# A two-layer graph network on Trainium2: GpSimd asks for free places in the ring of gathered rows by pairs of edge tiles, in place of groups of four

## What is computed

```python
h = X * rsqrt(deg_out)                                  # L0: convolution
agg = segment_sum(h[src], dst, N) * rsqrt(deg_in)
gX = relu(agg @ W) + relu(X @ Wres)
x = layernorm(X + batchnorm(gX))
h = x @ W_enc.T + b_enc                                 # L1: two layers
for l in range(2):
    m = relu(concat([h[src], h[dst]]) @ msg_W1[l].T + msg_b1[l])
    m = m @ msg_W2[l].T + msg_b2[l]
    agg = segment_sum(m, dst, N)
    h = layernorm(h + concat([h, agg]) @ upd_W[l].T + upd_b[l])
out = layernorm(x + h @ W_out.T + b_out)
```

## Time and profile before

| what | value |
| --- | --- |
| median of the three runs | 3993.59 us |
| lowest and highest of them | 3985.41 and 4000.14 us |
| span of the profiled execution (first to last instruction) | 3444.6 us |
| median less the span | 549.0 us |
| PE, PEld, DVE, ACT, POOL busy | 86%, 78%, 78%, 69%, 54% of the span |
| granted TensorE clock, mean | 0.971 |
| first edge stage, from GpSimd's first gather to its last | 544.5 to 1003.4 us |
| second edge stage, likewise | 1577.4 to 2101.3 us |
| third edge stage, likewise | 2532.3 to 3056.9 us |

### The profile page before, as it was taken

One profiled execution on the slowest core, in us unless ns is written; L12 is line 12 of the kernel. 1 busy time (PEld: TensorE's weight loads), 2 busy tenths in 40 slices (PEclk: granted clock), 3 DMA queues, 4 the chain that ended last, 5 costly groups with the idle time before them and its releaser, 6 DMA issues. The chain is left out here.

```text
span 3444.6 us, 92529 instructions
## 1 busy us (share of the span) xinstructions
PE 2975.2 (86%) x25312; PEld 2674.1 (78%) x25312; DVE 2700.0 (78%) x8634; ACT 2379.7 (69%) x5642; POOL 1846.0 (54%) x1782
## 2 busy tenths in 40 slices
PE   4975656777767789997999998999979999989998
PEld 3753334555543378987999998999979999989998
DVE  9999967888856688885777776666657777769998
ACT  3779945777742368886777775666657777759999
POOL 0000036577755533335776776555547767766664
PEclk9999988999979989999999999999989999999999
DMA  0027635777649989997776654999977766548887
GB/s 21 2 69 229 223 103 162 221 219 215 195 139 340 346 280 355 366 356 250 225 221 208 191 158 123 327 327 326 328 239 229 221 210 194 164 129 287 296 295 240
DMA packets 460711, 777.79 MB, mean 226 GB/s; under 512 B 113689, under 2 KB 115865, under 8 KB 460393
## 3 DMA queue, kind: packets, MB, share of 16 engines
q1 hardware_dynamic: 355046, 548.85, 48.2%
q10 hardware_dynamic: 67714, 147.73, 12.5%
q0 software_dynamic: 37632, 77.15, 9.2%
HBM read 451.50 MB, written 321.78 MB: 224 GB/s over the span
## 5 line engine op out<-in xcount | busy, mean ns | idle before, releaser
L883 DVE SCALAR_TENSOR_TENSOR edges_acc<-edges_acc,keep,edges_ps_a 128x128 f32 (+1 forms) x2352 | 820.3, 349 | 272.1 <-issue 145.9
L851 POOL DMA_INDIRECT ring<-table_p,esrc x784 | 787.5, 1004 | 313.3 <-issue 206.0
L1011 PE MATMUL edges_ps_m<-ring,ident 128*128 x3136 | 609.7, 276 | 33.8 <-POOLq L840 33.8
L1012 PE MATMUL edges_ps_m<-edges_q_ring,edges_turned 128*128 x3136 | 608.8, 276 | 0.0
L1011 PEld LDWEIGHTS edges_ps_m<-ring,ident 128*128 128x128 f32 x3136 | 478.6, 193 | 34.7 <-ACT edges_turned L967 17.7
L1012 PEld LDWEIGHTS edges_ps_m<-edges_q_ring,edges_turned 128*128 128x128 f32 x3136 | 478.8, 193 | 0.0
L979 ACT ACTIVATE edges_msg<-edges_ps_m 128x512 f32<-128x512 f32 x392 | 234.2, 597 | 295.5 <-PE edges_ps_m L1012 294.7
L1021 PE MATMUL edges_ps_a<-edges_onehot,edges_msg 128*128 128x128 f32 x3136 | 414.0, 275 | 0.0
L851 POOL DMA_INDIRECT ring<-table_h,esrc x344 | 327.7, 953 | 138.5 <-issue 93.5
L1021 PEld LDWEIGHTS edges_ps_a<-edges_onehot,edges_msg 128*128 128x128 f32 x3136 | 381.7, 192 | 0.0
L868 DVE TENSOR_TENSOR edges_onehot<-iota,drel 128x512 f32<-128x512 f16 x441 | 305.0, 692 | 96.1 <-PE edges_ps_a L1021 94.0
(11 more groups left out here) (315 smaller groups left out, 6776.2 us busy)
## 6 DMA issues: line engine op xcount, KB each, us to landing
table_z<-nodes_z_t SPq DMA_DIRECT2D x196, 256.0 KB, 5.0
table_p<-nodes_p_out SPq DMA_DIRECT2D x196, 256.0 KB
table_q<-nodes_q_out ACTq DMA_DIRECT2D x196, 256.0 KB
edges_q_ring<-table_q SPq DMA_DIRECT2D x196, 256.0 KB, 4.8
edges_d_ring<-table_d ACTq DMA_DIRECT2D x98, 512.0 KB
table_t<-edges_acc SPq DMA_DIRECT2D x196, 256.0 KB
nodes_in_a<-table_t SPq DMA_DIRECT2D x196, 256.0 KB
nodes_in_z<-table_z SPq DMA_DIRECT2D x196, 256.0 KB, 4.3
```

The source lines that it names most:

```text
L851: nc.gpsimd.indirect_dma_start(out=ring[:, e % RE * W:e % RE * W + P], out_offset=None, in_=table[:, :], in_offset=bass.IndirectOffsetOnAx ...
L883: nc.vector.scalar_tensor_tensor(out=to, in0=to, scalar=m.keep[:, s:s + 1], in1=ps_a[:, i % AR, where(j):where(j) + F], op0=ALU.mult, op1= ...
L1011: nc.tensor.matmul(to, m.ident[:], rows[j], start=True, stop=False)
L1012: last = nc.tensor.matmul(to, turned[:, i % QR, j * P:(j + 1) * P], slots[j], start=False, stop=True)
```

## The change

The table holds one number for each pair of edge tiles (`NPAIR` = 196) instead of one for each group of four (98), and is now called `pair_end`. GpSimd waits before each pair, for the pair that holds the same two places, 64 tiles back (`AHEAD`). The words are loaded every 24 pairs. The announcement to TensorE (`landed`) stays as it was, by fours. In `plan_stage` the arrays `bound`, `full`, `tf` and `ends` grow to 196 columns.

```diff
+NPAIR = TP // 2
+PW = -(-NPAIR // 3)
+AHEAD = 64
...
-                nc.gpsimd.iota(bound[:], pattern=[[4 * P, NCHUNK]], base=4 * P, channel_multiplier=0,
+                nc.gpsimd.iota(bound[:], pattern=[[2 * P, NPAIR]], base=2 * P, channel_multiplier=0,
...
-                link(nc.vector.tensor_scalar(tf[:, 0, :], ps_c[0:1, 2, 0:NCHUNK], float(TP - 1), -1.0, ALU.min, ALU.add))
+                link(nc.vector.tensor_scalar(tf[:, 0, :], ps_c[0:1, 2, 0:NPAIR], float(TP - 1), -1.0, ALU.min, ALU.add))
...
-                link(nc.vector.tensor_copy(ends[:, 1, 0:NCHUNK], tf[:, 1, :]))
-                link(nc.vector.tensor_scalar(ends[:, 2, 0:NCHUNK], ends[:, 1, 0:NCHUNK], 2, None, ALU.arith_shift_right))
-                link(nc.vector.tensor_scalar(ends[:, 3, 0:NCHUNK], ends[:, 2, 0:NCHUNK], 1, None, ALU.add))
-                for k, to in ((0, m.chunk_end), (3, m.tile_end)):
-                    pack(to[:, 0:EW], 10, [ends[:, k, :].rearrange("o (w j) -> o w j", j=3)[:, :, j] for j in range(3)], 10)
+                link(nc.vector.tensor_copy(ends[:, 1, 0:NPAIR], tf[:, 1, :]))
+                link(nc.vector.tensor_scalar(ends[:, 2, 0:NPAIR], ends[:, 1, 0:NPAIR], 2, None, ALU.arith_shift_right))
+                link(nc.vector.tensor_scalar(ends[:, 3, 0:NPAIR], ends[:, 2, 0:NPAIR], 1, None, ALU.add))
+                for k, to, w in ((0, m.chunk_end, EW), (3, m.pair_end, PW)):
+                    pack(to[:, 0:w], 10, [ends[:, k, 0:3 * w].rearrange("o (w j) -> o w j", j=3)[:, :, j] for j in range(3)], 10)
...
-                    last = nc.tensor.matmul(ps_c[:, 2, 0:NCHUNK], ones[0:K, :], full[:, k, :], start=k == 0, stop=k == 3)
+                    last = nc.tensor.matmul(ps_c[:, 2, 0:NPAIR], ones[0:K, :], full[:, k, :], start=k == 0, stop=k == 3)
...
                 for g in range(first, NCHUNK):
-                    if g >= RE // 4:
-                        k = g - RE // 4
-                        if k % 24 == 0:
-                            ends = load(mybir.EngineType.Pool, m.tile_end[0:1, k // 3:k // 3 + 8])
-                        pool.wait_ge(s_seg if degrees else s_pq, third(ends, k))
-                        pool.sem_inc(s_go, 1)
-                    for j in range(4):
-                        e = 4 * g + j
+                    for e in range(4 * g, 4 * g + 4):
+                        if e % 2 == 0 and e >= AHEAD:
+                            k = (e - AHEAD) // 2
+                            if k % 24 == 0 or e == 4 * first:
+                                ends = load(mybir.EngineType.Pool, m.pair_end[0:1, k // 24 * 8:k // 24 * 8 + 8])
+                            pool.wait_ge(s_seg if degrees else s_pq, third(ends, k))
+                            pool.sem_inc(s_go, 1)
                         nc.gpsimd.indirect_dma_start(
```

More of the change, by code:

```diff
@@ L529, in plan_stage @@
         cols = sb("cols", [K, 4, 4])
-        bound = sb("bound", [K, NCHUNK])
+        bound = sb("bound", [K, NPAIR])
         cnt_w = sb("cnt_w", [K, 4, P])
         ended, ended1, at_e = sb("ended", [K, 4, S]), sb("ended1", [K, 4, S]), sb("at_e", [K, 4, S], F16)
-        full = sb("full", [K, 4, NCHUNK])
+        full = sb("full", [K, 4, NPAIR])
         local_t = sb("local_t", [K, 4, P], F16)
@@ L537, in plan_stage @@
         ti = sb("ti", [1, 9, S], I32)
-        tf, ends = sb("tf", [1, 3, NCHUNK]), sb("ends", [1, 4, 3 * EW], I32)
+        tf, ends = sb("tf", [1, 2, NPAIR]), sb("ends", [1, 4, 3 * PW], I32)
         ps_c = pb("ps_c", 4)
@@ L621, in _ @@
                 nc.vector.memset(m.chunk_end[:], 0)
-                nc.vector.memset(m.tile_end[:], 0)
+                nc.vector.memset(m.pair_end[:], 0)
                 nc.vector.memset(m.slots[:], 0)
@@ L691, in _ @@
                 nc.vector.tensor_copy(m.slots[:, 0:NB], table[:, :, 1])
[L692 to L693 removed]
+                link(nc.vector.tensor_scalar(tf[:, 0, 0:NCHUNK], sen_row[0:1, 1:1 + TP].rearrange("o (c j) -> o c j", j=4)[:, :, 3], 1.0, None, ALU.add))
+                link(nc.vector.tensor_copy(ends[:, 0, 0:NCHUNK], tf[:, 0, 0:NCHUNK]))
                 dve.wait_ge(s_full, 1)
[L695 removed]
+                link(nc.vector.tensor_scalar(tf[:, 0, :], ps_c[0:1, 2, 0:NPAIR], float(TP - 1), -1.0, ALU.min, ALU.add))
                 link(nc.vector.scalar_tensor_tensor(out=tf[:, 1, :], in0=bound[0:1, :], scalar=1.0 / P, in1=tf[:, 0, :],
                                                     op0=ALU.mult, op1=ALU.add))
[L698 to L702 removed]
+                link(nc.vector.tensor_copy(ends[:, 1, 0:NPAIR], tf[:, 1, :]))
[3 more added lines that the diff above has]
+                    pack(to[:, 0:w], 10, [ends[:, k, 0:3 * w].rearrange("o (w j) -> o w j", j=3)[:, :, j] for j in range(3)], 10)
             @block.tensor
@@ L1505, in build @@
         m.steps, m.slots = sb("steps", [1, 2 * NB], I32), sb("slots", [1, NB + 4], I32)
[L1506 removed]
+        m.chunk_end, m.pair_end = sb("chunk_end", [1, EW + 7], I32), sb("pair_end", [1, PW + 7], I32)
         m.esrc, m.elocal = sb("esrc", [P, TP], I32), sb("elocal", [P, TP])
```

3 lines of the change are left out of this document (removed).

## The result

| | median | ratio to before | 95% interval |
| --- | --- | --- | --- |
| before, six runs beside it | 3987.50 us | 1 | |
| changed, six runs | 3962.23 us | 0.9926 | 0.9901 to 0.9952 |

The kernel became faster by 0.74%, some 25 to 29 us. The forecast was no change, 3992.1 us in 3977 to 4012, with a chance of 0.04 for what happened. It was wrong.

A forecast was written before the change was run, and what follows sets the result against it. The prediction took TensorE to bound the second and third edge stage, and GpSimd's gathers only the first one's end. Terms of -2.50, +1.04, 0 and 0 gave -1.46 us on 3993.59: 3992.1 us, range 3977 to 4012.

The forecast's parts named there:

- What bounds the kernel: Second and third edge stage: TensorE is the bound, busy 525.57 and 525.96 of 526 us, so earlier gathers gain nothing.
- terms that were 0 "under cover": Second and third edge stage: GpSimd's work was taken as hidden by TensorE's 525.6 us, so its shifts counted 0.
- a difference of over 20 us outside the span: Whole kernel: a sign listed as showing the forecast wrong, with no mechanism known for it.
- Earlier asking, -2.50 us: First edge stage's end: GpSimd gets two gathers further, 2 x 1.25 us, all of it reaching the stage's end.
- Boundaries at no cost on GpSimd: Edge stages: 82 more boundaries each run on GpSimd's sequencer, which is ahead of the gathers; cost 0.
- rival A: Edge stages: GpSimd's sequencer loses its lead and boundaries show as gaps, +31.6 us, 4025 us; chance 0.08.
- The plan stage, +1.04: Plan stage: wider operands on VectorE, which is on the path there, cost 1.04 us more.
- B: First edge stage's end: all 11.0 us of TensorE's waits vanish and its clock stays up, 3980 us; chance 0.06.
- C: Edge stages: a GpSimd stall without a releaser takes the gain, net +0.6 us, 3994 us; chance 0.12.
- D: Ring waits: the first pair's places come no sooner or the time is lost again, 3994.6 us; chance 0.06.
- The range: Whole kernel: 3977 to 4012 us, from the scatter of the runs, widened by two rivals.

The follow-up runs named there:

- plan_only: Changed kernel with its table by pairs, but GpSimd waits only once in four tiles, as before the change: ratio 1.0009 to before.
- head_eights: Changed kernel plus 96 gathers and 288 spare writes in the program's first stage, eight gathers in a row, then 24 writes: ratio 1.0087 to before.
- head_paced: Changed kernel plus 96 gathers in the program's first stage, each followed by three spare writes on GpSimd: ratio 1.0001 to before.
- eights: Changed kernel at depth 64, but GpSimd waits once in eight tiles, for the end of all eight: ratio 1.0895 to before.
- b_again: The kernel before the change, unchanged, run and profiled again beside itself: ratio 1.0004.
- a_again: The changed kernel, with no further edit, run and profiled again: ratio 0.9949 to before.
- head: Changed kernel plus 96 gathers issued one behind the other in the program's first stage, where nothing waits for them: ratio 1.0201 to before.

## Why the prediction was wrong

*What bounds the kernel.* The failed step is the first one, that TensorE is the bound of the second and third edge stage, "busy 525.57 and 525.96 of 526 us", so that "gathers that come earlier can't shorten anything". True of the profile, not of the executions of the later runs: in their traces these stages take 716 to 726 us for the same two kernels. All terms that were 0 "under cover" of TensorE's 526 us had no such cover.

*The sign of it stood in the table.* 549 us between the median and the span were booked as lying outside the first and last instruction. In the later profiled executions the time exceeds the span by 1.7 to 2.1 us. A gap of 14% should have been read as "this profile is of another execution than the ones timed"; the last sentence of the prediction, "a difference of over 20 us outside the span, for which I have no mechanism", was near it and looked in the wrong place.

*Earlier asking, -2.50 us.* The mechanism (a gather or two sooner at the end of the first stage) can't be found in the timed kind of execution: 25 to 29 us came, spread over three stages. What the runs put in its place is a mechanism that I had not listed as a rival: that GpSimd's waits cut its gathers into runs, and that shorter runs cost TensorE less. That the gain hangs on the waits is shown (`plan_only`), and that longer runs stop TensorE is shown (`head_eights` against `head_paced`, `eights`). That this is how pairs gain on fours is argued from the dose: in the second stage the idle time without a releaser is not clearly less (105 to 122 us with pairs, 105 and 120 with fours), and it is TensorE's busy time that is shorter.

*Boundaries at no cost on GpSimd.* Holds. Of the 492 boundaries of pairs behind tile 64 in the changed kernel's timelines, 233 have a gap of 0.32 us or less, 250 are waits of over 0.7 us for places, and only 9 lie between, where rival A's 0.67 would be.

*The plan stage, +1.04.* The pieces are about right: the `memset` of `ends` takes 0.72 us (forecast 0.71), an instruction on 196 columns 0.25 to 0.35 (0.27), the pack's two 0.49 for 66 words against 0.41 for 33. But the stage as a whole takes longer than in the profile read: its 48 gathers lie over TensorE's part, and the first gather of the edge stage starts at 568 to 574 us, not 544.5. Between the two kernels on one chip the stage differs by 0.3 us (its table is done at 566.5 us in `b_again` and at 566.8 in `a_again`), less than the 1.04.

*The rivals.* B gave the right side (3980 us), but by luck: its reason, TensorE's waits at the end of the first stage, is not where the time came from. It was held for 0.06. A, C and D were all built on the same profile, of the other kind.

*The range.* It rested on the scatter of the medians and on mechanisms of a microsecond each. The unknown 549 us had no share in it.

## What to carry to other kernels

Compare the span of a profile with the times before anything else is read from it; if they differ by far more than a second profile of the same kernel does (here 549 us against 2), the profile may show another kind of execution, and its busy shares prove nothing about the bound of the timed ones. An engine that issues indirect transfers one behind the other may cost others time even when nothing waits for them. Here it paid to let it run less far ahead and to stop it often: the changed kernel with a depth of 24 tiles runs at 0.981 of before (0.9765 to 0.9853), 3920.60 us against 3998.93, and its only further edit is `AHEAD = 24`. By the intervals 32 may be as good.

## What the runs showed of the hardware

- 96 gathers at 1.25 us each, of 64 KB, lengthen a stretch of pure TensorE, VectorE and ScalarE work that doesn't use them by 98.9 us. At 2.3 us each they cause no stop of TensorE (0.3 us without a releaser).
- TensorE goes on for some time before it stops, and it comes back late. In `head` the first gather starts at 30.1 us, and TensorE still gets through 63 matmuls from 60 to 65 us, but only 18 in the next 5. The last gather starts at 155.3 us, and there are 4 matmuls from 160 to 165 us, 16 in the next 5 us, and 88 in the 5 behind these.
- In the stops its matmuls start at whole multiples of 0.70 us from each other, within 0.07 us: 2.13, 1.41 and 2.80 us in the rows of the second edge stage above, and 36 of the 37 distances of over 0.5 us in `head` from 75 to 160 us.
- While it nearly stands, its granted clock is 0.50 (`head`, 100 to 125 us; 0.53 in the second edge stage from 1740 to 1800). Of the 196 us by which the second edge stage exceeds the 526, 141 are idle and 55 are more busy time, from the lower clock and from matmuls that stand alone: the 31 from 1740 to 1800 us take 0.27 us each, the 179 from 1820 to 1840 0.11.
- Half the bytes at the same number of rows change nothing: 0.9936 against 0.9926 and 0.9949, and the first accumulate no earlier.
- **Left open.** What between GpSimd's issue and TensorE's instruction stream is shared is not settled; all that the rows show is "issue" without a releaser. The queue q8, named instruction, carries 178 packets and 2.92 MB, in 0.3% of the time, in the profile read first and in the changed kernel's alike. Nor is it settled why one execution, the first profiled, had none of these stops; no later one was like it, and the effect of the change on such an execution wasn't measured. The executions of the later runs all come with a record of their span and clock; whether the recording has a share in the stops no run shows.
